# Four stages on four images: attention of two images, then one recurrence with two alternating chains, in place of one image at a time

## The chip, the cores and the metric

The kernel runs on one core of one Trainium2 chip. The core has TensorE (PE: matmuls, and PEld: weight loads), VectorE (DVE), ScalarE (ACT), GpSimd (POOL) and the DMA queues of SyncE (SP), ACT and POOL. The metric is the device time of one execution in microseconds (us). Lower is better.

## The reference

The input is x, four images (B) of 32 channels and 96 x 96 pixels, float32. Four layers follow each other, each on the normalised sum so far:

```
x = x + _L0_conv_ref(_gn(x), ...)   # block attention with halo
x = x + _L1_conv_ref(_gn(x), ...)   # LSTM
x = x + _L2_conv_ref(_gn(x), ...)   # deformable convolution
x = x + _L3_conv_ref(_gn(x), M)     # 8 x 8 block transform
```

`_gn` normalises each channel of each image over its pixels. L0 is attention: queries are 8 x 8 blocks, keys are the 14 x 14 window about them, 4 heads. L1 is an LSTM with 128 hidden units along the width: every image row is a sequence, so one image is 96 sequences with 96 steps, and a step needs the one before it:

```
g = xg + h @ W_hh.T
i, f, gg, o = jnp.split(g, 4, axis=-1)
c = jax.nn.sigmoid(f) * c + jax.nn.sigmoid(i) * jnp.tanh(gg)
h = jax.nn.sigmoid(o) * jnp.tanh(c)
```

L2 computes, from x, nine sampling places per pixel with offsets, gathers the four corners of each, weighs them and convolves the result. L3 multiplies each 8 x 8 block with a matrix from both sides.

## The kernel before

An image lies in SBUF on 128 partitions: 4 row groups (J) of 24 rows (R) times 32 channels. Every engine has its own hand-written instruction list, and semaphores tie the lists together. A list runs in order, so an instruction that waits holds up all behind it on its engine.

Per image p there are five stages. `attention(p)` goes through 24 steps U (`NU`), each with 6 blocks: on PE `fill` (scores), `turned_scores`, `sums` (probabilities times values, line 1287) and `project`; on DVE `row_max` and the splitting of float32 operands into bf16 parts; on ACT `exps`. The split operands go to DRAM and come back stacked (`store_k`, `store_q`, `load_stack` on SP). `lstm(p)` runs 96 steps, all 96 sequences of the image at once. One step is, on PE, `recurrence` (4 gates, line 1366, float32, which is two instructions each), then `inputs` for the next step (12 bf16 matmuls of 96 columns, lines 1354 to 1356); on ACT tanh (673), sigmoid (676), tanh of the cell (678); on DVE a product (1040), a sum (1044) and a product (1046) that gives `hist`, which `recurrence` of the next step reads. Every fourth step `linear` (1374) adds the output. `prepare(p)` writes the gather table of the image to DRAM (`sample_table`, five stores of 5.1 MB together), and computes offsets, indices and weights in three chunks (`pixel_math`). Then POOL gathers.

An image has 72 units (`UNITS`) of 128 pixels. For one unit POOL issues 9 indirect DMAs (line 525), into one of 6 buffers `got` (`RING`). DVE then runs `unit` (lines 802, 804, 806, 810: weigh, add, add, transpose), and PE runs `convolve` (1187) on a group of 6 units; DVE adds the group to the image. Only when DVE has run line 804 on a unit is its buffer free for the unit six later. `transform(p)` is L3, and it needs every unit of its image.

What sets the order: all lists loop over phases q, in the order transform(q-2), attention(q), lstm(q), prepare(q), and then the units that are left. The units of image q-1 are consumed in phase q. They are spread over it by `point`: a call at fixed places in each stage (6 + 72 in attention, 96 in lstm, 8 in prepare), which runs units up to a number given by the table `DUE`. By the table an attention takes the count from 7 to 31 (24 units), an lstm to 60 (29 units). The weighing of a unit on DVE therefore stands between the attention's or the LSTM's own instructions. Phase 0 has no units, and after phase 3 the last image has all of its 72 left.

Of the kernel before, what the change touches and what calls it, by code (L numbers as in the profile page):

```python
# [12 lines left out]
P = 128  # L13
# [29 lines left out]
LIN = 4  # L43
HIST = 8
# [13 lines left out]
GUNITS = 6  # L58
GROWS = GUNITS // NCOL
NGRP = UNITS // GUNITS  # L60
GN = GUNITS * BLK
RING = 6
# [53 lines left out]
STAGES = (("l3", 4, 4), ("pre", 6, 7), ("l0", 3 * NU, 31), ("l1", W, 60), ("prep", 8, 64))  # L116

def due_units(phase):

    if phase == 0:
        return [0] * sum(n for _, n, _ in STAGES)
    due, done = [], 0
    for name, n, upto in STAGES:
        if phase < B or name == "l3":
            due += [done + (upto - done) * (i + 1) // n for i in range(n)]
            done = upto
    return due + list(range(done + 1, UNITS + 1)) + [UNITS] * 6

DUE = [due_units(q) for q in range(B + 1)]
LAG_CONV = 2
LAG_ADD = 4

def network(nc, x_in, l0, l1, l2, l3, out):
# [9 lines left out]
    x_parts = nc.dram_tensor("x_parts", [P, 3, W, R], BF16, kind="Internal").ap()  # L146

    ctx = ExitStack()
    with ctx:
# [6 lines left out]
        x = sb("x", [P, 2, XR, W])  # L156
# [11 lines left out]
        ones = sb("ones", [P, W], BF16)  # L168
# [3 lines left out]
        cw = sb("cw", [P, NTAP, J * BLK])  # L172
        wout = sb("wout", [P, NTAP, J * C])
        obias = sb("obias", [P, 1])
        base = sb("base", [P, NCH, CH, NOFF])
# [6 lines left out]
        mean = sb("mean", [P, 4])  # L182
        rstd = sb("rstd", [P, 4])
        shift = sb("shift", [P, 4])
        stats = sb("stats", [P, 4, 6 * NGRP])
        index = sb("index", [P, NCH, CH, NTAP], I32)
        weight = sb("weight", [P, NCH, CH, NTAP, 4])
        got = sb("got", [P, RING, NTAP, 4 * C])
        red = sb("red", [P, 2, NTAP, 2 * C])
        samp = sb("samp", [P, 2, NTAP, C])  # L190
        turned = sb("turned", [P, 2, NTAP, GN])

        scratch = turned[:, :, :, :].rearrange("p a n w -> p (a n w)")
# [7 lines left out]
        with ExitStack() as a0:  # L201
# [8 lines left out]
            v = sb("v", [HKEYS, 2, NB * 2, J, HEADS, 2 * D], where=a0)  # L210
# [6 lines left out]
        with ExitStack() as a1:  # L217
            xs = sb("xs", [P, J, W, R], BF16, where=a1)
            xn = sb("xn", [P, 2, CHUNK, R], where=a1)
            part = sb("part", [P, 2, 3, CHUNK, R], BF16, where=a1)  # L220
            sig = sb("sig", [HID, 3 * W], where=a1)
            gc = sb("gc", [HID, 2, W], where=a1)
            prod = sb("prod", [HID, 2, W], where=a1)
            tcell = sb("tcell", [HID, W], where=a1)
            hist = sb("hist", [HID, HIST, W], where=a1)

# [1333 lines left out]
```

## Time and profile before

| what | us |
|---|---|
| three runs, median | 5408.45 |
| lowest and highest run | 5402.57, 5425.98 |
| the profiled execution | 5414.31 |
| its span, first to last instruction | 5412.5 |

The span falls into stages. The bounds are taken from the first instruction of each group normalisation (line 774, 16 times, from 9.0 to 5391.1 us):

| from, to (us) | stage | length | POOL instructions (a unit has 9 gathers and one more) |
|---|---|---|---|
| 9, 280 | attention 0 | 271 | none |
| 280, 666 | lstm 0 | 386 | none |
| 666, 757 | prepare 0 | 91 | 42 |
| 757, 1364 | attention 1 | 607 | 292 |
| 1364, 1847 | lstm 1 | 483 | 254 |
| 1847, 1995 | prepare 1 and the units left | 148 | 95 |
| 1995, 2051 | transform 0 | 56 | 32 |
| 2051, 2621 | attention 2 | 570 | 269 |
| 2621, 3105 | lstm 2 | 484 | 253 |
| 3105, 3312 | prepare 2, transform 1 | 207 | 130 |
| 3312, 3883 | attention 3 | 571 | 268 |
| 3883, 4368 | lstm 3 | 485 | 253 |
| 4368, 4572 | prepare 3, transform 2 | 204 | 125 |
| 4572, 5391 | units of image 3 | 819 | 586 |
| 5391, 5412 | transform 3 | 21 | none |

The page gives for each engine its busy time; over the whole span PE is busy for 2775.3 us (51%), DVE for 2142.2 (40%), ACT for 1054.6 (19%) and POOL for 2550.1 (47%). None is near its limit over the span, so the table of stages is the view to start with: in each stage another thing is the limit.
### The profile page before, as it was taken

What the parts mean: (1) busy time and instruction counts of PE and PEld (TensorE: products, weight loads), DVE (VectorE), ACT (ScalarE), POOL (GpSimd) and SP (SyncE); (2) the same over time, 40 slices, a digit from 0 to 9 for tenths busy, and PEclk for the clock granted to TensorE, in tenths of its full rate; (3) what the DMA queues carried; (4) which work ended last, traced back from release to release, by engine and by line L of the source; (5) the groups of instructions that cost most, each with busy time, mean ns of one, the idle gap of its engine ahead of it and who ended that gap; (6) DMA issues with size and microseconds to landing.
All of it is one profiled execution on the core that took longest, in us unless ns stands there. A gap on an engine that the chain in (4) does not pass through costs nothing.

```text
span 5412.5 us, 63956 instructions
## 1 busy us (share of the span) xinstructions
PE 2775.3 (51%) x24896; PEld 2286.7 (42%) x24896; DVE 2142.2 (40%) x4277; ACT 1054.6 (19%) x2365; POOL 2550.1 (47%) x2615
## 2 busy tenths in 40 slices
PE   6877735665566624666566642666566651000001
PEld 4767624454556513544465522454356541000001
DVE  5632244443433434444333353444343353222222
ACT  4622212221211202222211211222221110000000
POOL 1000064445355564444455565444355456777774
PEclk9855565555555655655555575556555575555555
DMA  5510024332211214332111123333121121111111
GB/s 170 147 31 1 1 80 126 97 115 52 58 36 38 77 44 124 109 106 73 53 44 36 39 80 110 98 112 90 44 55 38 35 77 54 52 50 47 47 47 40
DMA packets 191156, 369.96 MB, mean 68 GB/s; under 512 B 58864, under 2 KB 88688, under 8 KB 190848
## 3 DMA queue, kind: packets, MB, share of 16 engines
q0 software_dynamic: 82944, 170.04, 12.1%
q1 hardware_dynamic: 104952, 192.41, 11.8%
q8 instruction: 198, 3.24, 0.3%
q10 hardware_dynamic: 2960, 3.44, 0.2%
q14 instruction: 102, 0.84, 0.1%
HBM read 260.46 MB, written 104.33 MB: 67 GB/s over the span
## 4 chain that ended last, share of the span: by engine, by line
PE 27%; issue 26%; DVE 18%; POOL 12%; another core or an unknown queue 10%; ACT 5%; DMA 1%; SPq 0%; ACTq 0%; DVEq 0%; POOLq 0%
POOL got L525 12%; PE bank L1366 8%; PE bank L1287 5%; DVE got L802 3%; PE bank L1272 2%; PE bank L1258 2%; DVE red L804 2%; DVE prod L1040 2%; ACT sig L676 2%; PE bank L1222 2%; DVE mx L876 2%; PE bank L1235 2%; DVE gc L1044 1%; PE bank L1187 1%
## 5 line engine op out<-in xcount | busy, mean ns | idle before, releaser
L525 POOL DMA_INDIRECT got<-sample_table,index x2592 | 2536.6, 979 | 2797.5 <-DVE red L804 1280.0
L1366 PE MATMUL bank<-hist,whh 128*128 128x96 f32 x3040 | 756.7, 429 | 554.3 <-DVE hist L1046 414.5
L1366 PEld LDWEIGHTS bank<-hist,whh 128*128 128x128 f32 x3040 | 667.9, 323 | 644.4 <-DVE hist L1046 475.4
L1187 PE MATMUL bank<-turned,wout 128*128 128x192 f32 x864 | 234.4, 443 | 902.2 <-DVE turned L810 625.3
L802 DVE TENSOR_TENSOR got<-got,weight 128x1152 f32<-128x1152 f32 x288 | 389.8, 1353 | 660.1 <-DMA got<-sample_table,index 659.8
L1187 PEld LDWEIGHTS bank<-turned,wout 128*128 128x128 f32 x864 | 216.0, 275 | 916.4 <-DVE turned L810 596.7
L876 DVE TENSOR_REDUCE mx<-bank 128x2 f32<-128x392 f32 x576 | 298.9, 557 | 690.0 <-remote 428.9
L608 ACT ACTIVATE pt<-bank 98x512 f32<-98x512 f32 x576 | 336.3, 596 | 1040.6 <-remote 564.1
L1040 DVE TENSOR_TENSOR prod<-sig,gc 128x192 f32<-128x192 f32 x384 | 135.5, 353 | 992.6 <-ACT sig L676 535.6
L1287 PE MATMUL bank<-pt,v 98*16 98x64 f32 x9216 | 366.4, 277 | 313.5 <-issue 310.8
L1287 PEld LDWEIGHTS bank<-pt,v 98*16 98x16 f32 x9216 | 222.9, 120 | 443.8 <-issue 421.5
L1354 PE MATMUL bank<-xs,wa 128*128 128x96 bf16 x1536 | 381.8, 280 | 34.1 <-DMA xs<-x_parts 34.1
L1356 PE MATMUL bank<-ones,bw 96*128 96x96 bf16 x1536 | 379.5, 279 | 0.0
L1355 PE MATMUL bank<-xs,wb 128*128 128x96 bf16 x1536 | 379.4, 279 | 0.0
L1272 PE MATMUL bank<-qst,kst 98*98 98x128 bf16 x2304 | 268.7, 278 | 53.4 <-issue 49.4
L1272 PEld LDWEIGHTS bank<-qst,kst 98*98 98x98 bf16 x2304 | 239.9, 174 | 72.4 <-issue 63.6
L1354 PEld LDWEIGHTS bank<-xs,wa 128*128 128x128 bf16 x1536 | 241.0, 157 | 34.4 <-DMA xs<-x_parts 25.7
L1258 PE MATMUL bank<-kst,qst 96*128 96x196 bf16 x1152 | 215.1, 324 | 55.3 <-DVE mx L876 43.9
L676 ACT ACTIVATE sig<-bank 128x288 f32<-128x288 f32 x384 | 157.5, 410 | 427.4 <-PE bank L1366 314.1
L673 ACT ACTIVATE gc<-bank 128x96 f32<-128x96 f32 x384 | 96.5, 251 | 650.4 <-remote 274.8
L1355 PEld LDWEIGHTS bank<-xs,wb 128*128 128x128 bf16 x1536 | 221.4, 144 | 3.4
L804 DVE TENSOR_TENSOR red<-got 128x576 f32<-128x576 f32 x288 | 218.3, 758 | 9.9
(128 smaller groups left out, 3194.3 us busy)
## 6 DMA issues: line engine op xcount, KB each, us to landing
kst<-k_parts SPq DMA_DIRECT2D x96, 441.0 KB
got<-sample_table,index POOLq DMA_INDIRECT x2592
qst<-q_parts SPq DMA_DIRECT2D x96, 288.0 KB
k_parts<-kp SPq DMA_DIRECT2D x24, 882.0 KB
k_parts<-kp SPq DMA_DIRECT2D x24, 588.0 KB
q_parts<-qp SPq DMA_DIRECT2D x24, 576.0 KB
sample_table<-tab SPq DMA_DIRECT2D x8, 1568.0 KB
q_parts<-qp SPq DMA_DIRECT2D x24, 384.0 KB
```

Source lines behind the costliest of these rows:

```text
L525: pool.indirect_dma_start(out=got[:, uu % RING, n, :], out_offset=None, in_=tables[p], in_offset=bass.IndirectOffsetOnAxis(ap=at, axis=0)) ...
L608: act.activation(pt[:, n % SLOTS].rearrange("p a c n -> p (a c n)"), st_ps[n % SLOTS][0:HKEYS, :], ACT.Exp).then_inc(exp_done, 1)
L802: dve.tensor_tensor(corners, corners, w, ALU.mult).then_inc(weighted, 1)
L804: dve.tensor_tensor(red[:, par], got[:, slot, :, 0:2 * C], got[:, slot, :, 2 * C:4 * C], ALU.add).then_inc(reduced, 1)
L876: dve.tensor_reduce(mx[:, U % 2, j // 3, 2 * (j % 3):2 * (j % 3) + 2], s_ps[j % 2][:, 0:2 * KEYS].rearrange("p (k n) -> p k n", n=KEYS), A ...
L1187: mm = pe.matmul(out_ps[k % 2], wout[:, tap, :], turned[:, k % 2, tap, :], start=(tap == 0), stop=(tap == NTAP - 1))
L1272: mm = pe.matmul(st_ps[n % SLOTS][0:HKEYS, at:at + P], kst[0:ROWS + 2, U % KR, pair, blk, HKEYS * chunk:HKEYS * (chunk + 1)], qst[0:ROWS + ...
L1287: mm = pe.matmul(pv_ps[32 * h:32 * h + 2 * D, QS * blk:QS * (blk + 1)], v[:, G % 2, 2 * blk + chunk, j, h, :], pt[:, n % SLOTS, h // 2, ch ...
L1354: pe.matmul(dst, wa[:, w], xin, start=(n < 2), stop=False, skip_group_check=True)
L1355: pe.matmul(dst, wb[:, w], xin, start=False, stop=False, skip_group_check=True)
L1356: mm = pe.matmul(dst, bw[0:96, w], ones[0:96, :], start=False, stop=(t == 0), skip_group_check=True)
L1366: mm = pe.matmul(dst, whh[:, w], hist[:, (t - 1) % HIST, :], start=False, stop=True, skip_group_check=True)
```

## The change

The stages are put in another order, the same on every engine:

- before: A0 L0 P0 | A1 L1 P1 | T0 A2 L2 P2 | T1 A3 L3 P3 | T2, rest of the units, T3
- now: A0 A1, L(0,1), P0, A2, P1, A3, L(2,3), P2, 13 units, T0, T1, P3 (with 8 and 25 units between its chunks), 30 units, T2, the rest, T3

(A attention, L lstm, P prepare, T transform; | marks where a phase ends.) The two LSTM stages take two images each. Per time step the two images alternate on PE, ACT and DVE, each with its own buffers and semaphores. `inputs` now does two time steps at once, 12 matmuls of 192 columns, which is half as many instructions per image; the gates of both steps share two PSUM banks per image, so `inputs` of an image waits until the sigmoid of its last step is done. All four images stay in SBUF (`x` has B slots). To make room, `red` and `samp` have one buffer in place of two (DVE waits for the transpose of the unit before), `index` and `weight` are four slots for chunks across images, and `base` and `cw` are loaded again in every `prepare`, ahead of the halo rows on SP's queue. A convolution group is 3 units in place of 6, and two groups share one addition.

The table of units is now one list over the whole program. By it nothing is due until P0 is over; 42 units are due in A2, 10 in P1, 41 in A3, 35 in L(2,3), 9 in P2, and then one per point. POOL's own list is as before: 72 units of each image in order, each waiting for its buffer, its indices and its table.

```diff
-GUNITS = 6
+GUNITS = NCOL
+ADDS = 2
+SLOTS2 = 4
...
-STAGES = (("l3", 4, 4), ("pre", 6, 7), ("l0", 3 * NU, 31), ("l1", W, 60), ("prep", 8, 64))
+    stages = ((2 * (6 + 3 * NU) + W + TABLE_POINTS + 3, 0),
+              (6 + 3 * NU, 42), (TABLE_POINTS + 3, 52),
+              (6 + 3 * NU, 93), (W, 128), (TABLE_POINTS + 3, 137),
...
             def prepare(p):
...
+                sp.dma_start(base[:, :, :, :].rearrange("p m u n -> p (m u n)"), pix_base).then_inc(base_in, 16)
+                sp.dma_start(cw[:, :, :].rearrange("p t o -> p (t o)"), conv_w).then_inc(taps_in, 16)
...
                 for t in range(W):
-                    tt = W * p + t
-                    act.wait_ge(g_done, tt + 1)
-                    wait(act, prods_done, tt)
-                    act.activation(gc[:, 0, :], g_ps[t % 2][:, 0:W], ACT.Tanh).then_inc(g_act, 1)
...
+                    for a in range(2):
+                        act.wait_ge(g_done[a], tt + 1)
+                        wait(act, prods_done[a], tt)
+                        act.activation(gc[:, a, 0, :], gates[a][:, h:h + W], ACT.Tanh)
+                        act.wait_ge(ifo_done[a], tt + 1)
+                        wait(act, hid_done[a], tt)
+                        act.activation(sig[:, a, :, :], ..., ACT.Sigmoid).then_inc(ifo_act[a], 1)
+                        act.wait_ge(cell_done[a], tt + 1)
+                        act.activation(tcell[:, a, :], gc[:, a, 1, :], ACT.Tanh).then_inc(tanh_done[a], 1)
...
                 for t in range(W):
-                    if t > 0:
-                        recurrence(t)
-                    if t + 1 < W:
-                        inputs(t + 1)
-                    if t % LIN == 0 and t > 0:
-                        linear(t // LIN - 1)
-                    point(p)
+                    for a in range(2):
+                        if t > 0:
+                            recurrence(a, t)
+                        if t % LIN == 0 and t > 0:
+                            linear(a, t // LIN - 1)
+                        if a == 0 and t % 2 == 0 and t > 0:
+                            inputs(1, t)
+                        if a == 1 and t % 2 == 1 and t + 1 < W:
+                            inputs(0, t + 1)
+                    point()
```

Three places show how the lists change. The first is ACT in the LSTM. Before, one image's three activations of a step follow each other:

```order
L673 ACTIVATE gc<-bank 128x96
L676 ACTIVATE sig<-bank 128x288
L678 ACTIVATE tcell<-gc 128x96
L673 ACTIVATE gc<-bank 128x96
L676 ACTIVATE sig<-bank 128x288
```

Now the same three stand for image a = 0 and then for a = 1 of the same time step:

```order
L718 ACTIVATE gc<-gates 128x96
L721 ACTIVATE sig<-gates 128x288
L724 ACTIVATE tcell<-gc 128x96
L718 ACTIVATE gc<-gates 128x96
L721 ACTIVATE sig<-gates 128x288
L724 ACTIVATE tcell<-gc 128x96
```

So the first activation of one image stands behind the last of the other; six of them make one joint time step.

The second place is PE in the LSTM. Before, a step's four recurrence matmuls, and the first of the twelve input matmuls of 96 columns that follow:

```order
L1366 MATMUL bank<-hist,whh 128x96 x4
L1354 MATMUL bank<-xs,wa 128x96
L1355 MATMUL bank<-xs,wb 128x96
L1356 MATMUL bank<-ones,bw 128x96
L1354 MATMUL bank<-xs,wa 128x96
```

Now the recurrence of image 0, its `linear`, and the recurrence of image 1 and of image 0's next step together (x8), before the inputs for two steps (192 columns):

```order
L1450 MATMUL gates<-hist,whh 128x96 x4
L1459 MATMUL bank<-hist,wlin 32x96 x4
L1450 MATMUL gates<-hist,whh 128x96 x8
L1438 MATMUL gates<-xs,wa 128x192
L1439 MATMUL gates<-xs,wb 128x192
L1440 MATMUL gates<-ones,bw 128x192
L1438 MATMUL gates<-xs,wa 128x192
```

Inputs are issued once per joint step, in turn for one image and the other, and each time for two steps of that image.

The third place is DVE in an attention that runs beside gathers, near the end of a group of blocks. Before, one unit (its first instruction is line 802) with the row maxima (876) of a whole step U up to the next unit:

```order
L802 TENSOR_TENSOR got<-got,weight 128x1152
L804 TENSOR_TENSOR red<-got 128x576
L806 TENSOR_TENSOR samp<-red 128x288
L810 STREAM_TRANSPOSE turned<-samp 128x9x32
L885 TENSOR_SCALAR mparts<-bank 12x128
L887 SCALAR_TENSOR_TENSOR mparts<-bank,mparts 12x128
L895 COPY osb<-bank 128x6x8x8
L876 TENSOR_REDUCE mx<-bank 128x2 x6
```

Now the next unit (854) comes after four maxima (935) and one subtraction:

```order
L854 TENSOR_TENSOR got<-got,weight 128x1152
L856 TENSOR_TENSOR red<-got 128x576
L859 TENSOR_TENSOR samp<-red 128x288
L863 STREAM_TRANSPOSE turned<-samp 128x9x32
L935 TENSOR_REDUCE mx<-gates 128x2 x4
L920 TENSOR_TENSOR kp<-k,kp 128x1176
L854 TENSOR_TENSOR got<-got,weight 128x1152
```

A step U holds one unit before, and one or two now.

## Rows read from the trace of the kernel before

**Rows 1.** The page, part 2: POOL's busy tenths in 40 slices of the span

```profile
POOL 1000064445355564444455565444355456777774
```

**Rows 2.** Busy time by stretch: from:to, length, PE, PEld, DVE, ACT, POOL (instructions), PEclk, DMA share, GB/s

```profile
9.00:280.00 271.00, 204.97 (x3676) 164.23 (x3676) 165.76 (x314) 140.76 (x251) 13.11 (x17) 0.91 0.50 149
280.00:666.00 386.00, 297.29 (x2108) 269.03 (x2108) 102.65 (x338) 99.75 (x300) 0.00 (x0) 0.50 0.04 12
666.00:757.00 91.00, 45.73 (x166) 28.79 (x166) 53.81 (x110) 17.74 (x31) 41.84 (x42) 0.76 0.29 88
2051.00:2621.00 570.00, 334.81 (x3766) 248.06 (x3766) 245.78 (x430) 141.68 (x250) 259.69 (x269) 0.58 0.34 95
2621.00:3105.00 484.00, 307.31 (x2180) 280.16 (x2180) 190.67 (x464) 97.75 (x300) 239.67 (x253) 0.53 0.17 43
```

**Rows 3.** Waits over the span: engine and line, releaser, us, times, longest

```profile
POOL got L525 <- DVE red L804: 1280.0, 155, 40.2
POOL got L525 <- DVE index L1120: 671.6, 1, 671.6
```

**Rows 4.** Busy time of three steps U of attention: image 0, then twice image 2

```profile
254.20:261.20 7.00, 5.18 (x137) 4.05 (x134) 6.83 (x14) 4.44 (x8) 0.00 (x0) 0.90 0.02 3
2553.90:2571.20 17.30, 10.02 (x134) 6.97 (x132) 9.79 (x17) 4.48 (x8) 7.14 (x9) 0.50 0.12 32
2571.20:2597.00 25.80, 10.63 (x120) 6.17 (x120) 3.56 (x7) 2.53 (x5) 17.50 (x18) 0.50 0.17 47
```

**Rows 5.** Timeline, PE, attention 2 during a gather: start, us, what, idle before

```profile
2223.66 0.31 PE L1287 MATMUL bank<-pt,v 98*16 98x64 f32 x2 [0.53 <-issue]
2224.37 0.26 PE L1287 MATMUL bank<-pt,v 98*16 98x64 f32 x1 [0.40 <-issue]
```

**Rows 6.** Waits between 9 and 280 us

```profile
PE bank L1177 <- DMA base<-pix_base: 22.0, 1, 22.0
```

**Rows 7.** Timeline of one LSTM step of image 0, no gathers

```profile
402.21 0.41 ACT L676 ACTIVATE sig<-bank 128x288 f32<-128x288 f32 x1 [1.03 <-PE bank L1366]
...
402.86 0.28 PE L1356 MATMUL bank<-ones,bw 96*128 96x96 bf16 x1
...
403.41 0.28 ACT L678 ACTIVATE tcell<-gc 128x96 f32<-128x96 f32 x1 [0.79 <-DVE gc L1044]
403.73 0.26 DVE L1046 TENSOR_TENSOR hist<-sig,tcell 128x96 f32<-128x96 f32 x1 [0.35 <-ACT tcell L678]
...
404.04 2.02 PE L1366 MATMUL bank<-hist,whh 128*128 128x96 f32 x8 [0.42 <-DVE hist L1046]
404.82 0.25 ACT L673 ACTIVATE gc<-bank 128x96 f32<-128x96 f32 x1 [1.12 <-PE bank L1366]
...
405.86 0.29 PE L1354 MATMUL bank<-xs,wa 128*128 128x96 bf16 x1
...
406.10 0.41 ACT L676 ACTIVATE sig<-bank 128x288 f32<-128x288 f32 x1 [1.03 <-PE bank L1366]
```

**Rows 8.** Timeline, ACT, LSTM of image 2 beside gathers

```profile
2736.01 0.41 ACT L676 ACTIVATE sig<-bank 128x288 f32<-128x288 f32 x1 [1.03 <-PE bank L1366]
...
2741.02 0.41 ACT L676 ACTIVATE sig<-bank 128x288 f32<-128x288 f32 x1 [2.10 <-PE bank L1366]
...
2773.20 0.25 ACT L673 ACTIVATE gc<-bank 128x96 f32<-128x96 f32 x1 [4.73 <-remote]
2775.35 0.41 ACT L676 ACTIVATE sig<-bank 128x288 f32<-128x288 f32 x1 [1.90 <-remote]
```

**Rows 9.** Groups by line, POOL: first 4597 to 4813 us, then 4887 to 5341

```profile
L525 POOL DMA_INDIRECT got<-sample_table,index x172 | 165.0, 959 | 52.4 <-issue 52.4
...
L525 POOL DMA_INDIRECT got<-sample_table,index x325 | 338.5, 1042 | 116.3 <-issue 116.3
```

**Rows 10.** Timeline of the end: POOL's last gather, and the last addition

```profile
5364.26 0.95 POOL L525 DMA_INDIRECT got<-sample_table,index  x1 [0.30 <-issue]
...
5390.29 0.36 DVE L816 TENSOR_TENSOR x<-bank,x 128x192 f32<-128x192 f32 x1 [20.38 <-remote]
```

More of the change, by code:

```diff
@@ L260, in network @@
         o_ps = bank[3:5]
[L262 removed]
+        x_loaded = [[sem(f"x_loaded{p}{i}") for i in range(3)] for p in range(B)]
         consts_in = sem("consts_in")
@@ new lines, in point, with points @@
+            def point():
+                nonlocal point_count, units_done, adds_done
+                i = point_count
+                point_count += 1
+                while units_done < DUE[i]:
+                    unit(units_done)
+                    units_done += 1
+                while adds_done < B * NADD and ADD_AT[adds_done] <= i:
+                    add_rows(adds_done)
+                    adds_done += 1
+            def points(n):
+                for i in range(n):
+                    point()
@@ L1057, in lstm @@
-                add_linear(W // LIN - 1)
+                        record(p, 2, k, image(p)[:, :, 4 * LIN * k:4 * LIN * (k + 1)])
+                for a in range(2):
+                    combine(2 * pair + a, 1, 6)
+                for a in range(2):
+                    dve.memset(gc[:, a, 1, :], 0.0).then_inc(cell_zero[a], 1)
+                for k in range(2):
+                    for a in range(2):
+                        columns(k, a)
+                    for a in range(2):
+                        rest_part(k, a)
+                    for a in range(2):
+                        last_part(k, a)
@@ L1059, in prepare @@
+                for a in range(2):
+                    add_linear(W // LIN - 1, a)
             def prepare(p):
@@ L1357, in inputs @@
-                        if t == 0 and n in (0, 3):
-                            mm.then_inc(g_done if n == 0 else ifo_done, 1)
-                def recurrence(t):
-                    tt = W * p + t
-                    pe.wait_ge(hid_done, tt)
+                        pe.matmul(gate(a, n), wa[:, w], xin, start=(n % 2 == 0), stop=False, skip_group_check=True)
+                        pe.matmul(gate(a, n), wb[:, w], xin, start=False, stop=False, skip_group_check=True)
+                        mm = pe.matmul(gate(a, n), bw[0:96, w], ones[0:96, :], start=False, stop=(first == 0), skip_group_check=True)
@@ L1395, in prepare @@
+                    point()
+                for a in range(2):
+                    pe.wait_ge(hid_done[a], W * (pair + 1))
+                    linear(a, W // LIN - 1)
             def prepare(p):
```

713 lines of the change are left out of this document (380 added, 333 removed).

## The prediction

> **What bounds the kernel now.** I read the 40 slices first: POOL's row is all but empty for the first five slices and then stands between 3 and 6 tenths until the last six or seven, where it is at 7 [rows 1]. A gather engine that is needed for all four images is idle at the start and half idle in the middle. The waits say why: POOL waits 671.6 us for the first indices, and 1280.0 us in 155 pieces for DVE to free a buffer [rows 3]. Then the stretches [rows 2]. The time is a sum of stages, and each has its own limit. Attention without gathers took 271 us, with 24 units beside it 570. An LSTM without gathers took 386, with 29 units 484. Only in the last 819 us is POOL itself the limit.
>
> Why attention doubles is seen in three rows. With gathers PE issues in small bursts, one to three matmuls every 0.71 us, and waits for nothing that is named in between [rows 5]. A step U of 7.0 us becomes 17.3 with one unit gathered (x9), and a step with two (x18) takes 25.8, though it holds less other work [rows 4]. And the granted clock falls from 0.91 to 0.58 [rows 2]. So a gather costs attention much, whoever it belongs to, and an attention that has none beside it is cheap. The LSTM is a chain: one step is 3.89 us (402.21 to 406.10), in which every engine waits for another [rows 7]. Beside gathers I saw steps of 5.01 us, the sigmoid 1.1 us late, and, once in some 13 steps, one that is 4.5 us longer because ACT starts late (4.73 us of idle time) [rows 8].
>
> **The change part by part.** I rebuild the span of 5412.5 us stage by stage, up to the end of L(2,3), and then count what POOL has left.
>
> Head 9, A0 271: as before. PE's 22.0 us wait for constants [rows 6] loses two loads (base, cw) but the front gains two images of x, so I leave it.
>
> A1 now follows A0 with no gather beside it. It is A0 less the 22.0 us wait, plus some 6 for the normalisation behind A0's last addition: 271 - 22 + 6 = 255. It was 607.
>
> L(0,1): a joint step has two limits. ACT runs gc, sig, then waits for DVE's two products, then tcell, and only then the other image's gc: from sig to the end of tcell is 403.41 + 0.28 - 402.21 = 1.48 us, with gc 0.25 and a gap some 1.78 per image [rows 7], so 3.6 per joint step. PE needs per image 1.82 for the recurrence (404.04 to 405.86) and, for twelve input matmuls, 402.86 + 0.08 less 401.97 (405.86 minus one period of 3.89), 0.97; with linear 2.8, so 5.6 per joint step at the 1.2 GHz level (the row says 0.50 [rows 2]) and 2.8 at 2.4 GHz. Which level? The rows show A0 at 0.91 and L0 at 0.50 [rows 2]. In L0 PE waited for `hist` in every step; in the joint step at 1.2 GHz it would wait for nothing, as in A0's dense stretches. I take the higher level and 3.65 us: 96 x 3.65 = 350, plus 24 for two normalisations and the first columns, plus 21 for the second image's splitting work and the end: 395. Bounds: 385 and 575 (96 x 5.6 + 37). Two images for the price that one had (386).
>
> The Trainium skill (page "TensorE: Matmul & The Clock Gate", section "Part 1: The HAM clock gate") says the low clock is the default and activity releases it. By it alone the joint step would be 3.65 us; by the L0 row alone (0.50 at 297 busy of 386) it would be 5.6. The traces bear out both halves, since A0 has 0.91.
>
> P0: 91, as before [rows 2]. The base and cw loads and then the halo rows stand ahead on SP; the offset matmuls that need cw come over 10 us later, so at most 5 us. First gather at 9 + 271 + 255 + 395 + 36 = 966 us (before 702.7, after 671.6 us of waiting [rows 3]).
>
> A2 with 42 units, A3 with 41, in place of 24 each. DVE has 18 more units, each 3 us of DVE, and 18 more gathers stream past. The marginal price of a second gather in a step U is 25.8 - 17.3 = 8.5 us [rows 4], with some DVE time on top: I take 9. The other bound is the average price, (570 - 265) / 24 = 12.7. A2 = 570 + 18 x 9 = 732, A3 = 571 + 17 x 9 = 724. POOL needs 42 x 11.3 to 12.6, about 500 us, so it isn't the limit there.
>
> P1: as P0, with 10 units of which 6 lie ready in the ring: 100.
>
> L(2,3) with 35 units: streams run for some 350 us of it. In a stream both images' sigmoids are 1.1 late, so a joint step is 3.65 + 2.2 = 5.85, and 60 steps go there; 36 steps x 3.65 = 131 are outside; 24 for the head; DVE's 35 units cost 3 us each, of which half is hidden: 50. ACT's late starts: 13 steps of 3 activations become 6.5 joint steps of 6, so 15 x 4.5 = 67. Sum 350 + 131 + 24 + 50 + 67 = 622, rounded 620. Bounds: 500 (all late starts hidden) and 760 (PE too is slowed in the stream, as in attention).
>
> The Trainium skill (page "Runtime: NRT & Kernel Launch", section "Instruction fetch mechanics") says instruction memory is refilled in blocks ahead of use and mostly hidden. No stall stands in L0, but the regular late start of ACT beside gathers [rows 8] looks like such a refill coming late. If the rule held beside gathers too, my 67 us would go (a rival, below).
>
> The sum to the end of L(2,3): 9 + 271 + 255 + 395 + 91 + 732 + 100 + 724 + 620 = 3197. By then DVE has consumed 128 units by the table, POOL is at most six ahead: 134. So 154 units are left, and from here POOL is the limit: P2, T0, T1 and P3 consume 33 units by the table in less than the 370 us or so that POOL needs for these, and six buffers (70 us) carry it over the stretches without a unit. POOL's pace has two values: 216 us / 172 x 9 = 11.3 us per unit, and later in the same stage 454 / 325 x 9 = 12.57 [rows 9]. The first held for some 30 units of unbroken gathering, then the second set in. I take 30 x 11.3 + 124 x 12.57 = 1898. After the last gather starts, 5412.5 - 5364.3 = 48 us remain, 20.4 of them the wait before the last addition [rows 10]; these stay.
>
> 3197 + 1898 + 48 = 5143 us, which is 270 less than 5412.5. Around the span lie 1.8 us (5414.3), and the median is 6 below the profiled run: 5140.
>
> Costed at nothing: the single buffers `red` and `samp` (DVE runs its list in order anyway, and the wait for its own transpose is covered by that order) and the smaller convolution groups (the same columns on PE).
>
> **The rivals.**
>
> (a) Attention pays the average price for each extra unit, 12.7 us: A2 799, A3 787, so 130 more, 5270. For it: U with one unit costs 10.3 more than the 7.0 of image 0, plus clock. Against: the step with two.
>
> (b) The LSTM stays at 1.2 GHz: L(0,1) 575 (+180), L(2,3) at PE's 5.6 outside the streams (+70): 5390, the same as before within half a per cent.
>
> (c) Slower: the chains don't overlap. Every list is in order; if ACT or PE stands at image 0's wait while image 1 is ready, a joint step costs two single ones. L(0,1) 772 (+377), L(2,3) 968 (+348): 5865. It decides from where the two joint stages cost 1015 + 297 = 1312 us, 6.5 us per joint step, for 5440. Against: DVE and ACT are idle for most of a single step [rows 7].
>
> (d) POOL keeps 11.3 us per unit to the end: 154 x 11.3 = 1740, 158 less: 4980. For it: it did for 30 units. Against: the later, longer row [rows 9].
>
> (e) No late starts of ACT in L(2,3): 67 less, 5075.
>
> **How the numbers follow.** Forecast 5140: 0.58. (a) 0.13, (b) 0.06, (c) 0.07, (d) 0.12, (e) 0.04. The range takes in all but (b) and (c), with the costs' own bounds: low 4930 (d, and attention at 8.5 with L(2,3) at 580), high 5330 (a with L(2,3) at 680). Half a per cent, 27 us, is about what a measurement of this kernel can tell. Faster: forecast, (a), (d), (e) make 0.87; (b) is the same, 0.06; (c) slower, 0.07.
>
> **What the profile after would show.** First gather near 966 us. A1 near 255 us at a clock near 0.9. L(0,1) near 395 with a clock above 0.8; a clock of 0.5 there means (b), and steps near 7.8 us mean (c). A2 and A3 near 730. L(2,3) near 620, with ACT idle for 4 to 5 us some 15 times. POOL's row at 7 or more from about 3200 us on, with no wait for DVE over 10 us; waits there would mean that the table gives DVE its units too late, and my 1898 is too short. 48 us behind the last gather.

## The result, and the profile after

| what | us |
|---|---|
| the changed kernel, median of 4 runs | 5239.41 (5222.64 to 5260.03) |
| the kernel before, median of 4 runs beside them | 5405.51 (5396.03 to 5425.98) |
| ratio, 95% interval | 0.969 (0.9644 to 0.9735) |
| the profiled execution and its span | 5222.64, 5220.7 |

It is 3.1% faster. The forecast was 5140, with 4930 to 5330 as its range, so the sign and the range held, and the middle was 99 us too low: a gain of 270 us was forecast and one of 166 came.

The runs of this study came in two settings. In one of them (here called **setting 1**: the runs above, e5 to e7, e11, e12) the kernel before took 5405 to 5480 us, in the other (**setting 2**: e1 to e4, e8 to e10) the same kernel took 4337 to 4348. The setting doesn't go with the chip's number, which was 15 in e1 to e4 (setting 2) and in e11 (setting 1). What follows compares within a setting, or says that it doesn't. Within setting 1 the kernel before still varied by 1.4% between series, so a stage is best compared with a run whose kernel before took about the same.

The stages of the changed kernel, from group normalisation to group normalisation, as busy time in windows. The columns are the window, its length, then for PE, its weight loads (PEld), DVE, ACT and POOL the busy time and the number of instructions, then the granted clock, the DMA share and GB/s. They answer to [rows 2].

```profile
9.00:288.00 279.00, 204.91 (x3676) 162.96 (x3676) 168.58 (x320) 138.68 (x251) 13.12 (x17) 0.90 0.49 151
288.00:543.00 255.00, 205.26 (x3676) 164.11 (x3676) 163.18 (x314) 136.70 (x249) 0.00 (x0) 0.76 0.48 143
543.00:906.00 363.00, 311.25 (x3064) 286.27 (x3064) 202.82 (x676) 170.97 (x597) 0.00 (x0) 0.96 0.09 24
906.00:973.00 67.00, 45.92 (x166) 29.02 (x166) 41.72 (x94) 17.72 (x31) 23.61 (x24) 0.83 0.38 121
973.00:1705.00 732.00, 358.52 (x3911) 262.73 (x3911) 291.71 (x496) 140.85 (x250) 403.83 (x409) 0.58 0.31 87
1705.00:1830.00 125.00, 56.62 (x220) 37.74 (x220) 72.00 (x136) 17.82 (x31) 80.78 (x77) 0.70 0.31 93
1830.00:2515.00 685.00, 375.09 (x3929) 276.93 (x3929) 291.07 (x495) 140.38 (x250) 367.03 (x374) 0.56 0.32 89
2515.00:3186.00 671.00, 454.30 (x3282) 406.55 (x3282) 308.45 (x826) 174.91 (x597) 307.16 (x318) 0.74 0.17 44
3186.00:5221.00 2035.00, 364.43 (x1536) 302.47 (x1535) 590.07 (x913) 59.38 (x102) 1388.32 (x1392) 0.54 0.20 54
```

| stage | forecast | measured |
|---|---|---|
| A0, A1 | 271, 255 | 279, 255 |
| L(0,1) | 395 | 363 |
| P0 | 91 | 67 |
| A2 | 732 | 732 |
| P1 | 100 | 125 |
| A3 | 724 | 685 |
| L(2,3) | 620 | 671 |
| end of L(2,3) | 3197 | 3186 |
| from there to the end | 1946 | 2035 |

Up to the end of L(2,3) the sum is off by 11 us of 3197, though single stages are off by up to 51. The rest of the miss is the last stretch, 89 us. The waits of POOL and DVE there (engine, tile and line, what was waited for; us in total, times, longest), from 3186 to the end. They answer to [rows 3], but for the last stretch alone. POOL's:

```profile
POOL got L565 <- issue: 434.6, 1371, 15.6
POOL got L565 <- DVE red L856: 160.9, 21, 34.5
```

DVE's waits in the same stretch:

```profile
DVE turned L863 <- remote: 575.4, 20, 41.3
DVE got L854 <- DMA got<-sample_table,index: 450.5, 60, 9.4
DVE turned L863 <- issue: 123.3, 3, 41.3
DVE x L1211 <- remote: 78.2, 2, 61.0
```

DVE stood for 575.4 + 123.3 = 699 us, in 23 pieces, ahead of a transpose into `turned` (line 863), and six buffers later POOL stood for DVE, for 160.9 us. I had written that no such wait would be over 10 us. `turned` has two buffers; the first unit of a group waits there until PE has convolved the group before the last. And PE had done so long ago, by its row. The timeline of both engines in such a place (start, busy us, engine, line, what, idle time before and its releaser). PE's rows:

```profile
4350.63 4.13 PE L1262 MATMUL bank<-turned,wout 128*128 128x96 f32 x18 [84.45 <-issue]
4357.03 3.94 PE L1262 MATMUL bank<-turned,wout 128*128 128x96 f32 x17 [2.28 <-DVE turned L863]
4362.98 0.32 PE L1262 MATMUL bank<-turned,wout 128*128 128x96 f32 x1 [2.00 <-issue]
```

DVE's rows from there on, with the units in between left out:

```profile
4349.76 0.48 DVE L863 STREAM_TRANSPOSE turned<-samp 128x288 f32<-128x288 f32 x1 [41.32 <-remote]
4350.16 0.32 DVE L869 TENSOR_TENSOR x<-bank,x 128x192 f32<-128x192 f32 x1
...
4359.04 0.46 DVE L859 TENSOR_TENSOR samp<-red 128x288 f32<-128x288 f32 x1
4400.16 0.48 DVE L863 STREAM_TRANSPOSE turned<-samp 128x288 f32<-128x288 f32 x1 [40.66 <-remote]
...
4450.56 0.48 DVE L863 STREAM_TRANSPOSE turned<-samp 128x288 f32<-128x288 f32 x1 [41.32 <-remote]
```

### The profile page after: what moved, and what is told of

It is laid out like the page before. It is cut to its first block, busy times and chain, and to the rows that moved or that the text cites. A ratio compares the mean times of both kernels' runs of the same rounds, so it can differ in the third digit from the quotient of the medians.

```text
span 5220.7 us, 60707 instructions
## 1 busy us (share of the span) xinstructions
PE 2376.3 (46%) x23456; PEld 1928.8 (37%) x23456; DVE 2133.6 (41%) x4275; ACT 997.4 (19%) x2358; POOL 2584.3 (50%) x2615
## 4 chain that ended last, share of the span: by engine, by line
another core or an unknown queue 28%; issue 20%; PE 19%; DVE 15%; POOL 9%; ACT 3%; DMA 1%; SPq 0%; DVEq 0%; ACTq 0%; POOLq 0%
POOL got L565 9%; PE gates L1450 4%; DVE got L854 3%; PE bank L1368 3%; DVE mx L935 2%; PE bank L1262 2%; DVE red L856 1%; PE gates L1339 1%; ACT sig L721 1%; DVE prod L1106 1%; DVE samp L859 1%; PE bank L1303 1%; PE gates L1353 1%; PE gates L1438 1%
## 5 line engine op out<-in xcount | busy, mean ns | idle before, releaser
L1262 PE MATMUL bank<-turned,wout 128*128 128x96 f32 x1728 | 346.7, 376 | 1356.2 <-issue 740.5
L1450 PE MATMUL gates<-hist,whh 128*128 128x96 f32 x3040 | 481.5, 309 | 185.9 <-DVE hist L1112 98.9
L1450 PEld LDWEIGHTS gates<-hist,whh 128*128 128x128 f32 x3040 | 433.2, 219 | 223.5 <-DVE hist L1112 124.7
L935 DVE TENSOR_REDUCE mx<-gates 128x2 f32<-128x392 f32 x576 | 298.4, 556 | 508.7 <-remote 279.3
L1368 PE MATMUL bank<-pt,v 98*9 98x64 f32 x9216 | 313.6, 263 | 270.6 <-issue 269.9
L863 DVE STREAM_TRANSPOSE turned<-samp 128x288 f32<-128x288 f32 x288 | 137.8, 478 | 710.2 <-remote 575.4
L648 ACT ACTIVATE pt<-gates 98x512 f32<-98x512 f32 x384 | 225.8, 596 | 710.6 <-remote 398.7
L1339 PE MATMUL gates<-kst,qst 96*128 96x196 bf16 x1152 | 205.3, 306 | 77.0 <-DVE mx L935 47.8
L1438 PE MATMUL gates<-xs,wa 128*128 128x192 bf16 x768 | 211.9, 276 | 53.9 <-ACT sig L721 24.4
L1440 PE MATMUL gates<-ones,bw 96*128 96x192 bf16 x768 | 211.9, 276 | 1.4 <-issue 1.4
L1439 PE MATMUL gates<-xs,wb 128*128 128x192 bf16 x768 | 210.4, 274 | 2.4 <-issue 2.4
```

What stands on the lines that cost most here:

```text
L648: act.activation(pt[:, n % SLOTS].rearrange("p a c n -> p (a c n)"), st_ps[n % SLOTS][0:HKEYS, :], ACT.Exp).then_inc(exp_done, 1)
L935: dve.tensor_reduce(mx[:, U % 2, j // 3, 2 * (j % 3):2 * (j % 3) + 2], s_ps[j % 2][:, 0:2 * KEYS].rearrange("p (k n) -> p k n", n=KEYS), A ...
L1262: mm = pe.matmul(out_ps[n % 2][:, at:at + GN], wout[:, tap, :], turned[:, k % 2, tap, :], start=(tap == 0), stop=(tap == NTAP - 1))
L1339: mm = pe.matmul(s_ps[j % 2][:, KEYS * k:KEYS * (k + 1)], qst[0:ROWS, U % KR, j // 3, blk].rearrange("p s q -> p (s q)"), kst[0:ROWS, U % ...
L1368: mm = pe.matmul(pv_ps[32 * h:32 * h + D + 1, QS * blk:QS * (blk + 1)], v[:, G % 2, 2 * blk + chunk, j, h, :], pt[:, n % SLOTS, h // 2, ch ...
L1438: pe.matmul(gate(a, n), wa[:, w], xin, start=(n % 2 == 0), stop=False, skip_group_check=True)
```

## The experiments

**Theories.** R (rate): beside gathers PE works slowly, and it is PE that limits the last stretch. L (lag): PE's answer comes a fixed time late, and two buffers are too few. I (idle): PE is slow since it idles at the low clock. G, added after the first four: PE is slowed by gathers in setting 1 and not at all in setting 2, and that is the difference between them.

**e1: four buffers** for `turned` in place of two, and PE's sums in two banks, from unit 204 on (the last 84 of the 288 units). Of the edit, the main lines:

```diff
+            more = sb("more", [P, 2, NTAP, GN], where=a3)
...
-                    wait(dve, convolved, k - 1)
...
+                    elif k >= FOUR + 4:
+                        dve.wait_ge(convolved, k - 3)
...
-                    wait(pe, rows_added, n)
+                    wait(pe, rows_added, n if k < FOUR + 2 else n - 1)
```

> From unit 204 on, DVE has four turned buffers in place of two, and PE's two sums lie in two banks, so PE need not wait for DVE's last addition. Three theories on the waits for turned (575 us in the changed kernel, 26 to 44 us at every third unit of the last stages), which let POOL pause. Theory R (rate): beside gathers PE works off a group of 18 fp32 matmuls in some 50 us, while POOL brings three units in 34 us, so PE is the limit there. Theory L (lag): PE's answer only comes some 45 us late, and two buffers are too few for that. Theory I (idle): PE is slow because it stands idle at the low clock between groups. R expects at most 20 us of gain, with DVE still waiting for PE in the stretches 4250 to 4450 and 4600 to 4930; L expects these waits gone and the time 50 to 75 us lower than the changed kernel (5239), so about 5170; I agrees with R here. Ratio to before: R 0.966 to 0.970, L 0.956.

**e2: one burst for six units** from unit 204 on (18 matmuls of 192 columns, as the kernel before has them).

```diff
+                if n >= SIX:
+                    if k % ADDS == 0:
+                        return
...
+                        mm = pe.matmul(out_ps[n % 2], wout[:, tap, :], big[:, n % 2, tap, :], start=(tap == 0), stop=(tap == NTAP - 1))
```

> From unit 204 on, two groups of 3 units are convolved in one burst of 18 matmuls of 192 columns, half as many instructions on PE for the same columns. Theory R, if the rate is one of instructions: 18 matmuls in some 50 us for 68 us of gathers, so PE is not the limit, DVE's waits for turned are gone from unit 204 on and the time is 50 to 75 us lower than the changed kernel: 5165 to 5190, ratio 0.957. If the rate is one of columns, a burst takes 100 us, and nothing changes (5239, ratio 0.969). Theory L expects the waits gone too, since the buffers hold twice the units.

**e3: more work for PE** from unit 204 on; nobody reads its result.

```diff
+                if n >= 34:
+                    for i in range(24):
+                        pe.matmul(bank[7][:, 0:2 * W], wa[:, 0:HID], ones[:, :], start=True, stop=True)
```

> From unit 204 on, PE runs 24 more bf16 matmuls of 192 columns ahead of each group (into a bank that nobody reads), so that it isn't idle for so long. Theory I expects a higher clock, the waits for turned gone and 50 to 75 us less than the changed kernel (about 5175). Theory R expects PE to be slower still for each group: at some 2.8 us per matmul and its weight load, 24 more are up to 67 us per group, for 28 groups up to 1900 us more; at a price per column they cost a quarter of it. Theory L expects no change (5239), as the 24 need 4 to 7 us of the 34.

**e4: units taken out of two stages**, by the table and two calls of `points` (18 behind attention 2, 35 behind L(2,3)); the table's edit:

```diff
-              (6 + 3 * NU, 42), (TABLE_POINTS + 3, 52),
-              (6 + 3 * NU, 93), (W, 128), (TABLE_POINTS + 3, 137),
+              (6 + 3 * NU, 24), (18, 42), (TABLE_POINTS + 3, 52),
+              (6 + 3 * NU, 93), (W, 93), (35, 128), (TABLE_POINTS + 3, 137),
```

> 18 of the 42 units due in attention 2 and all 35 units due in lstm(2,3) are taken out of these stages and stand in points of their own behind them. It measures the price of a unit beside other work. My working had 9 us per unit in attention (rival 12.7): attention 2 goes from 732 to 570 (rival: 503). Lstm(2,3), 671 measured with 35 units, goes to the 363 of lstm(0,1), at a clock near 0.97 and without ACT's late starts of 4 to 5 us, if these come from gathers; if they come from ACT itself they stay. In the open a unit costs 11.3, and six are ready in the ring: 12 x 11.3 = 136 and 29 x 11.3 = 328 come back. Sum with 9 per unit: 5239 - 162 + 136 - 308 + 328 = 5233, the same; with 12.7: 5140.

Measured, all four in setting 2, beside 4346.05 us of the kernel before: e1 4393 (ratio 1.0105, 1.0087 to 1.0124), e2 4398 (1.0129, 1.0111 to 1.0148), e3 4388 (1.0103, 1.0066 to 1.0141), e4 4665 (1.0738, 1.0714 to 1.0761). No expectation had this. The three that equal the changed kernel up to unit 204 are 1% *slower* than before. e4 is 272 us slower still than e1: where POOL is the limit, units taken out of a stage only stop it. It stands for DVE once for 310.8 us, in L(2,3), where DVE takes no units (the wait in e4; us in total, times, longest):

```profile
POOL got L565 <- DVE red L856: 340.3, 29, 310.8
```

Stages of e1 (same columns as above): A2, A3, L(2,3), and the stretch from P3 on.

```profile
976.00:1461.00 485.00, 291.34 (x3910) 239.92 (x3910) 291.54 (x494) 140.54 (x250) 373.98 (x365) 0.63 0.43 125
1577.00:2066.00 489.00, 295.82 (x3928) 243.58 (x3928) 289.56 (x493) 140.39 (x250) 375.64 (x373) 0.62 0.44 125
2069.00:2568.00 499.00, 391.54 (x3277) 360.95 (x3277) 307.84 (x823) 171.11 (x597) 348.06 (x349) 0.84 0.23 63
2848.00:4359.00 1511.00, 236.88 (x1016) 207.91 (x1016) 458.00 (x667) 23.78 (x41) 1150.17 (x1185) 0.52 0.20 56
```

A2 takes 485 us where setting 1 has 732. The stages without gathers are the same: L(0,1) is 361 us and the first gather comes at 945, against 363 and 942.5. So it isn't that all is faster, and this bears G out as far as PE goes. POOL's waits over the whole of e1:

```profile
POOL got L575 <- DVE index L1206: 907.2, 1, 907.2
POOL got L575 <- issue: 781.2, 2543, 6.5
POOL got L575 <- DVE red L866: 53.7, 48, 6.5
```

From its first gather to its last POOL is the limit: 4358.7 - 945.1 = 3413.6 us for 288 units, 11.85 each. And of PE's semaphores none in e1 is over 0.6 us late, beside gathers or not (0.75 us in all seven traces of setting 2). In setting 2 the time is the first gather plus what POOL needs; the change moves the first gather from about 703 us (so in both traces of the kernel before, which are of setting 1; there is none of setting 2) to 945 us, and what it saves POOL later doesn't make up for it. Since PE is on time there, e1 to e3 say nothing of R, L and I, but each of them takes away one cause of slowness *for setting 2*: buffers, burst size and PE's load change nothing.

**e5, e6: before and changed, unchanged**, to test G.

> The kernel before, unchanged, for its trace. In the first four experiments the kernel before took 4346 us, not 5405, and in their traces PE's semaphores come 0.01 us behind the end of a matmul also beside gathers, where in the traces of before and of the changed kernel they come up to 50 us late. If that is all of the difference (theory G: beside gathers PE is slowed in one place and not in the other), the stages without gathers take the same time here as in the first trace (attention 0 271, lstm 0 386, prepare 0 91, first gather near 703), attention beside gathers takes about 480 in place of 570 to 607, and POOL is at 7 tenths and more nearly throughout. The rival (theory E: everything is faster here) has the first gather well before 650. A time near 5405 would mean that the first condition is back.

> The changed kernel, unchanged. Theory G: where PE is not slowed, POOL is the limit from the first gather on, so the time is first gather + 288 units x 11.3 = 3254 + 100 to 150 of POOL's own slow units + some 31 behind the last gather: 945 + 3254 + 160 + 31 = 4390 us, 1% slower than before (4346), since its first gather comes 240 us later. Rival: the changed kernel keeps its 3% lead (4211). If the kernel before takes 5405 again, the changed one takes 5239.

These came in setting 1: e5 5481.95, e6 5319.54 beside 5480.01 (0.9696, 0.9649 to 0.9744). So the result holds a second time, neither run tests G, and the condition of e6's 4390 was not met; that number stays untested on the changed kernel itself, and rests on e1 to e3. The stages of e5 are close to those of the first trace: A0 274, L0 386, P0 92, attention 1 615 (607). In e6 L(0,1) took 363 as before, and A2, A3 and L(2,3) took 761, 699 and 697, where the first trace of the changed kernel had 732, 685 and 671.

**e7: the two chains take turns.**

```diff
                     pe.wait_ge(hid_done[a], tt)
+                    pe.wait_ge(hid_done[1 - a], tt + a)
```

> The two chains of the joint LSTM are tied: on PE the recurrence of each image also waits for the other image's last hidden state, so a joint step is two single steps behind each other. It measures what the overlap of the chains is worth. My working: joint step 3.65 overlapped, 2 x 3.9 = 7.8 tied, so lstm(0,1) goes from 360 to about 755 us; rival (the overlap was small, and a joint step is short for another reason, the inputs of two steps at once): below 500. Lstm(2,3) grows by at most as much. Where POOL is the limit, the first gather moves from 945 to 1340 and the whole by the same 395 us: 4785; L(2,3) then costs nothing as long as POOL has units.

Setting 1, 5751.75 (1.0496, 1.0473 to 1.0518). The two joint stages:

```profile
555.00:1226.00 671.00, 449.25 (x3060) 397.05 (x3060) 203.82 (x671) 195.15 (x596) 0.00 (x0) 0.74 0.05 13
2887.00:3693.00 806.00, 512.59 (x3276) 453.63 (x3276) 308.65 (x822) 193.26 (x596) 298.08 (x313) 0.67 0.14 36
```

Counted from the second normalisation, as here, L(0,1) is 671 in place of 360 and L(2,3) 806 in place of 694 (e6). Without the overlap a gain of 3% becomes a loss of 5%: 5752 - 5320 = 432, of which 311 and 112 are the two stages. The granted clock of L(0,1) fell too, from 0.97 to 0.74, since PE waits more; the run doesn't part the two. My price for tied chains was too high, though: in the trace a tied pair takes 5.97 us and the next one 7.68, in turns, so 6.8 and not 7.8. My 7.8 was twice 3.89, a step of L0 at a clock of 0.50.

**e8, e9: e2's and e4's kernels again**, for setting 1; they came in setting 2.

> The same kernel as e2_six: from unit 204 on, one burst of 18 matmuls of 192 columns for 6 units, in place of two of 18 with 96 columns. In e2 PE's semaphores were not late, so it told nothing of the waits. Where they are late (kernel before near 5400 to 5480), theory R with a rate of instructions expects DVE's waits for turned gone from unit 204 on (some 4220 us on) and 50 to 75 us less than the changed kernel: ratio to before 0.957. If the rate is one of columns, a burst takes 100 us of 68, PE stays the limit and the ratio is 0.969 as for the changed kernel. Theory L (a fixed lag of 45 us) expects the waits gone too; e1's kernel tells L from R.

> The same kernel as e4_shift: 18 units out of attention 2, all 35 out of lstm(2,3), each set in points of their own behind the stage. Where PE's semaphores are late, attention 2 goes from 732 (5239 us) or 761 (5320 us) down by 18 x 9 = 162, or by 18 x 12.7 = 229 by the rival. Lstm(2,3) has no gathers but for the six that fill the ring, so theory G (gathers slow PE) has it at 375 with a clock near 0.95, from 671 to 694: a marginal price of 8.5 to 9 us per unit. The whole: the 136 and 328 us of gathers in the open come back, and PE's late answers beside them may hold DVE there too (up to 16.8 us per unit, 50.4 us for three): 0 to +250 on the changed kernel.

Measured 4388.6 (1.009, 1.0068 to 1.0112) and 4663.41 (1.0725, 1.0703 to 1.0746), the same as e2 and e4. Their conditions weren't met, and they show only that the setting's times repeat.

**e10, e11: a kernel with a trial in each stretch.** e4's table, then e2's burst (units 204 to 227), e3's extra matmuls (228 to 257), e1's buffers (258 to 287). Each is read in its own stretch and not by the whole time.

> One kernel with a trial in each stretch; it is read stage by stage, not by its whole time. (1) 18 units out of attention 2 and 35 out of lstm(2,3), as in e4. (2) Units 204 to 227 with one burst of 18 matmuls of 192 columns for 6 units. (3) Units 228 to 257 with 24 more bf16 matmuls of 192 columns ahead of each group of 3. (4) Units 258 to 287 with four turned buffers, and PE's sums in two banks. If PE's semaphores come late beside gathers here: (1) attention 2 takes 732 - 162 = 570 at 9 us per unit, or 503 at 12.7, and lstm(2,3) about 375. (2) Theory R by instructions: a burst is done within 50 us of its start, and the stretch runs at 11.3 us per unit without DVE waits for turned; by columns: 100 us, and waits stay. (3) Theory I: the bursts are done within 5 us and no waits for turned; theory R: over 50 us per group, with the stretch slower than in the changed kernel. (4) Theory L: no waits for turned; theory R: PE's semaphores still 50 us apart, and the waits come back after the four buffers are full. If they are not late here, all stretches run at 11.3 us per unit.

> The same kernel as e10_stretches, where PE's semaphores were not late and all stretches ran at 11.3 us per unit. Where they are late: (1) attention 2 takes 570 us at 9 us per unit, or 503 at 12.7, and lstm(2,3) about 375. (2) One burst for 6 units: by instructions done within 50 us of its start and no DVE waits for turned; by columns 100 us, and waits stay. (3) 24 more matmuls per group: theory I has the bursts done within 5 us; theory R over 50 us per group and a slower stretch. (4) Four buffers: theory L has no waits for turned; theory R has PE's semaphores still 50 us apart, and the waits back once the four are full.

e10 came in setting 2 (4642.88 beside 4336.68; from unit 204 on the units are 11.3 to 11.4 us apart, and DVE never waits for `turned`). e11 came in setting 1 (5455.78 beside 5462.73). Two windows of e11 (columns as above): A2 up to its last exponential, and L(2,3) without units.

```profile
991.00:1515.00 524.00, 302.07 (x3754) 228.76 (x3754) 231.27 (x407) 137.35 (x247) 225.79 (x236) 0.61 0.35 99
2591.00:2957.00 366.00, 314.98 (x3078) 290.24 (x3078) 202.00 (x670) 170.83 (x596) 3.78 (x4) 0.96 0.09 25
```

The *attention price*. Up to the same place the changed kernel takes 722 us in its first trace (kernel before 5405) and 752 in e6 (5480, nearer to e11's 5463):

```profile
973.00:1695.00 722.00, 354.26 (x3846) 260.76 (x3846) 285.69 (x486) 137.90 (x246) 403.83 (x409) 0.58 0.31 88
976.00:1728.00 752.00, 376.88 (x3846) 272.01 (x3846) 286.56 (x485) 137.58 (x247) 398.81 (x407) 0.55 0.30 84
```

DVE has weighed 42 units there, and 24 in e11, so a further unit costs (722 - 524) / 18 = 11.0 us, or (752 - 524) / 18 = 12.7: rival (a)'s 12.7 rather than my 9, in this stage. (A unit is nine POOL instructions, without the tenth that I gave it ahead of the prediction: from the first gather to the last, POOL's row holds 2592 gathers for 288 units and nothing else.)

The *LSTM*: without gathers L(2,3) is L(0,1) (366, clock 0.96). ACT's waits in it:

```profile
ACT tcell L746 <- DVE gc L1141: 150.2, 192, 2.1
ACT sig L743 <- PE gates L1494: 16.6, 82, 0.6
ACT gc L740 <- PE gates L1494: 13.0, 22, 3.7
```

The same in L(2,3) of the changed kernel:

```profile
ACT tcell L724 <- DVE gc L1110: 159.1, 138, 4.2
ACT gc L718 <- remote: 158.7, 41, 10.0
ACT sig L721 <- remote: 55.8, 32, 4.6
```

ACT's late starts are gone without gathers, and in e1, with gathers but with PE on time, there is no "remote" for ACT either. So the late starts were PE's late semaphores, 73 of them for 214.5 us, and not ACT.

*The last stretches of e11.* (2) one burst for six: units 204 to 225 came 11.4 us apart, DVE waited for nothing but gathers, and a burst of 18 matmuls was answered 26 us after its start. (3) extra matmuls: DVE waited 111.7 us for `turned` in two pieces, the longest 74.3, at a clock of 0.55 (0.53 in stretch 2, 0.50 in stretch 4). Theory I falls: more work raised the clock by little and didn't make PE quick. (4) four buffers: DVE got past the transposes but stood at the addition, as its waits from 5043 to 5416 show:

```profile
DVE got L876 <- DMA got<-sample_table,index: 139.3, 17, 9.4
DVE x L900 <- remote: 137.9, 2, 72.2
```

And here PE shows its pace, since two groups were queued behind each other (PE in the timeline of e11):

```profile
5103.65 0.32 PE L1306 MATMUL bank<-more,wout 128*128 128x96 f32 x1 [2.47 <-issue]
5106.45 0.32 PE L1306 MATMUL bank<-more,wout 128*128 128x96 f32 x1 [2.48 <-issue]
5109.25 0.32 PE L1306 MATMUL bank<-more,wout 128*128 128x96 f32 x1 [2.48 <-issue]
5112.05 0.32 PE L1306 MATMUL bank<-more,wout 128*128 128x96 f32 x1 [2.48 <-issue]
```

One matmul each 2.80 us. 18 of them are 50.4 us, which is the time from one answer to the next in the changed kernel. This is R, and L (a fixed lag) falls: from 0.01 to 50 us is no fixed time, and what is queued together is answered one behind the other. But 2.80 us is no fixed price of a matmul either: in stretch 2 eighteen with twice the columns were answered in 26 us, 1.4 each, and what sets the pace is open. It isn't instructions that come late: PE has about this pace from 5048 to 5129, and between 5043 and 5175 the gathers' queue is the only one that moves anything, the queues of instructions nothing.

```profile
q0 software_dynamic: 3014, 6.19, 17.7%
```

A group for three units thus costs PE 50.4 us in the worst stretches, and POOL brings three units in 34.

**e12: e2's kernel as a whole in setting 1.**

> The kernel of e2_six and e8_six_again once more, for its whole time where PE's semaphores are late. In e11 the stretch with one burst for 6 units ran 21 units at 11.4 us each with no wait for turned. In the changed kernel POOL pauses and is slow for 103 us from unit 204 on, some 30 of it behind transform 2, which stay. So 50 to 75 us less than the changed kernel: ratio to before 0.957 where the kernel before takes 5400 to 5480. If DVE then waits elsewhere instead (for the burst at the addition), the ratio stays at 0.969. Where PE's semaphores are not late it is 1.009 to 1.013 again.

5234.36 beside 5411.38: 0.9683 (0.966 to 0.9706). The 50 to 75 us that I expected did not come. DVE's waits for `turned` from unit 204 on are gone (from 4100 us on they were 467 us in the changed kernel), yet the last gather comes at 5183 in place of 5169. 25 us of that were lost ahead of unit 204, where the kernels are the same. From unit 204's first gather to the last one, three traces of this part of the changed kernel (the first, e6, e7) have 1048.3, 1048.1 and 1050.4 us and e12 has 1037.5, so what the wider bursts gain is 11 us. The waits of DVE from 4100 us to the end of e12:

```profile
DVE got L861 <- DMA got<-sample_table,index: 655.1, 76, 10.1
DVE x L1227 <- remote: 110.7, 3, 51.7
DVE x L885 <- remote: 20.1, 1, 20.1
```

Two windows of e12 (columns as above):

```profile
4543.00:4794.00 251.00, 21.61 (x72) 20.43 (x72) 72.14 (x100) 0.00 (x0) 190.79 (x198) 0.53 0.20 52
4833.00:5133.00 300.00, 21.27 (x72) 19.98 (x72) 76.10 (x104) 0.00 (x0) 227.85 (x215) 0.53 0.18 47
```

251 / 198 x 9 = 11.4 us per unit, then, after some 250 us without a pause, 300 / 215 x 9 = 12.6: the slow pace of [rows 9] is back. The changed kernel, whose POOL was made to pause, shows it only in single units. And transform 2 (line 1227) waits for PE longer, 110.7 us against 16.5. Taking DVE's wait away let POOL run unbroken, and unbroken it is slower in this setting. In setting 2 the pace stays at 11.3 to 11.4 to the end, in all seven traces (from unit 216 on 24 units take 272 to 277 us, and the last 23 take 260 to 265). So I don't read 12.6 as POOL's own price, but what slows it is as open as what slows PE. G is thus not the whole difference between the settings: PE is late in one and not in the other, and POOL's slow pace too is in one alone.

## Why the prediction was right, and where it was off

- **What bounds the kernel** was right in kind: cheap attentions ahead of the first gather, one joint recurrence for two, more units under the work. A1 255 (255); its clock was 0.76 and not near 0.9, at the same length.
- **L(0,1): 363 for 395.** The step was 3.56 on average against 3.65, and the clock 0.96, as I chose; rivals (b) and (c) fall by this row, and e7 shows that it rests on the overlap. The 21 us for the second image's splitting work don't exist: it lies beside the first steps. That activity releases the low clock, as the Trainium skill has it ("TensorE: Matmul & The Clock Gate", "Part 1: The HAM clock gate"), held in the direction that I used: 0.96 here, 0.50 in L0.
- **P0: 67 for 91**, since part of its work runs into the next stage; the first gather came 36 us into it as before, at 942.5 against 966 forecast.
- **A2: 732 for 732, by luck.** I took 24 units as the load of the stage before, from the table; between the same marks DVE weighed 27 there. So 15 more were added and not 18, and they cost (732 - 570) / 15 = 10.8 us each and not 9: 15 x 10.8 = 18 x 9. In A3, 685 for 724, 14 more units cost (685 - 571) / 14 = 8.1 each. The same stages took 761 and 699 in e6, so 9 is a fair mean, good to some 3 us in a single stage. Rival (a)'s average has the same wrong count, and its 265 stands in no row: (570 - 255) / 27 is 11.7.
- **L(2,3): 671 for 620**, inside its bounds. The term that fell is ACT's late starts, 67 us. I read a wait on ACT as ACT's own. It was PE's late semaphores, and they cost far more: e11's stage without gathers is 366, e1's with gathers and a punctual PE 499 (setting 2), so, across the settings, the units beside it cost some 133 and PE's lateness 172. By the Trainium skill ("Runtime: NRT & Kernel Launch", "Instruction fetch mechanics") instructions are fetched in blocks ahead of use, mostly hidden. Nothing here contradicts it: no such stall is left where PE is on time.
- **The last stretch: 2035 for 1946**, the mis-sized term. Its working was 11.3 for 30 units and 12.57 for 124, 157 us over the bare 11.3. Measured: 2035 - 154 x 11.3 - 52 behind the last gather = 243 over it, 161 of them waits for DVE; the other 82 I haven't resolved. The step that failed is "POOL is the limit from here": PE was, for stretches of 100 to 300 us. Rival (d) had the pace between the pauses nearly right, and not the pauses. I had costed the smaller convolution groups at nothing, "the same columns on PE"; but [rows 10] had shown DVE waiting 20.38 us for "remote" where only PE's last group was left to come, and [rows 5] PE in bursts each 0.71 us with nothing to wait for. Both fit a late PE, and I had not asked what they meant for a group. What smaller groups cost by themselves is nonetheless little, 11 us by e12: most of what they lose in waits, POOL gives back in pace.
- The 52 us behind the last gather were 48 in the forecast.
- **What I could not have seen**: in setting 2 the same change costs about 1%, by e1 to e3. My bottleneck view has the reason (the first gather comes 240 us later), but the traces had no setting in which POOL alone decides.

## What to carry to other kernels

A wait that ends with no instruction's end, above all behind a matmul, is a wait for PE even when PE's row says idle: compare the release with the row's end before you blame the waiting engine. When a wait is taken away and the time stays, look whether the engine that was held up now runs at a slower pace of its own. And a change that delays the start of a resource, to make the work beside it cheaper, wins only while that work is the limit; say which of the two it is, since it can differ between runs of one kernel.

## What the runs showed of the hardware

- One and the same kernel took 5405 to 5480 us in some runs and 4337 to 4348 in others, and the stages without indirect gathers took the same in both (L(0,1) 363 us in the changed kernel and 361 in e1). What sets it is open; the DMA packets of the gathers took the same time in both (122.1 to 126.5 and 121.8 to 125.7 ns on average).
- In the slower setting PE, beside gathers, gave its answers up to 50 us late, and in e11 with a full queue it issued one fp32 matmul of 96 columns each 2.80 us, while a burst of 18 with 192 columns was answered in 26 us.
- There, POOL's gathers went from 11.4 to 12.6 us per unit after some 250 us without a pause (e12); in the other setting they didn't in 1500 us (e1, from 2848 to 4359).
- 24 more matmuls of 192 columns in some 34 us, beside gathers, left the granted clock at 0.55, against 0.50 and 0.53 in the stretches of e11 without them.
